# Two cross attentions of a perceiver: the first rebuilt with all heads' queries on partitions, the second reordered around its transposes and maxima

## The reference, cut to what matters

```python
# layer 0: scores = q k / 4 + mask * -1e9, softmax over the 1024 keys, times v, @ Wo.T + bo
qh = split_heads(layernorm(x) @ Wq.T + bq)          # 16 batches, 16 heads, 64 queries, 16 features
kh = split_heads(ctx @ Wk.T + bk)                   # 16 batches, 16 heads, 1024 keys, 16 features
vh = split_heads(ctx @ Wv.T + bv)
attn = softmax(einsum('bhqd,bhkd->bhqk', qh, kh) / sqrt(16) + mask * -1e9)
x = x + merge_heads(einsum('bhqk,bhkd->bhqd', attn, vh)) @ Wo.T + bo
# layer 1: the same without a mask, then causal self attention and an fp4 feed forward
```

## Time and profile before

| | us |
|---|---|
| device time, median of 3 runs | 1369.87 (1366.11 to 1375.72) |
| device time of the profiled execution | 1370.36 |
| its span in the profile | 1368.3 |
| mean granted TensorE clock, as a share of the full one | 0.983 |
| TensorE busy | 1229.0 (90%) |
| VectorE busy | 951.4 (70%) |
| ScalarE busy | 857.8 (63%) |
| POOL busy | 660.1 (48%) |

### The profile page before, as it was taken

The page is one execution under the profiler, slowest core; times in us unless marked ns, Lnnn a source line. Parts: engine busy times, 40 slices in busy tenths (PEclk is TensorE's granted clock), DMA queues, the critical chain, the costliest instruction groups (busy, mean ns, idle before and its releaser), DMA issues. The chain is left out here.

```text
span 1368.3 us, 32530 instructions
## 1 busy us (share of the span) xinstructions
PE 1229.0 (90%) x12656; PEld 887.8 (65%) x12658; DVE 951.4 (70%) x1543; ACT 857.8 (63%) x1373; POOL 660.1 (48%) x897
## 2 busy tenths in 40 slices
PE   6999999999999988897978999998889998988886
PEld 3666767676777765554645667676667676766654
DVE  3787886787777773684676776676756677756674
ACT  3766767667777754543546667676768676767331
POOL 1665555455565642340013446355654657746533
PEclk9999999999999999999999999999999999999998
DMA  4311322111112203001633021002001132000000
GB/s 157 100 55 55 124 61 77 55 56 55 55 56 85 95 2 115 1 1 31 200 115 88 32 63 54 32 33 63 32 33 54 45 81 64 32 2 2 5 9 19
DMA packets 32853, 78.49 MB, mean 57 GB/s; under 512 B 4416, under 2 KB 16448, under 8 KB 28480
## 3 DMA queue, kind: packets, MB, share of 16 engines
q1 hardware_dynamic: 32704, 76.42, 18.2%
HBM read 69.07 MB, written 7.34 MB: 56 GB/s over the span
## 5 line engine op out<-in xcount | busy, mean ns | idle before, releaser
L697 POOL TENSOR_TENSOR ca_fold<-ca_probT 128x512 f32<-128x512 f32 x128 | 164.0, 1281 | 235.9 <-ACT ca_probT L927 235.4
L936 ACT ACTIVATE ca_probT<-bank 128x512 f32<-128x512 f32 x256 | 140.2, 595 | 110.8 <-PE bank L830 109.5
L801 PE MATMUL bank<-ca_kT,ca_q_blk 32*128 32x512 f32 x512 | 146.4, 648 | 9.7 <-DVE ca_probT L1016 7.1
L830 PE MATMUL bank<-ident,ca_prob 128*128 128x128 f32 x1024 | 144.5, 282 | 11.0 <-DVE ca_picked L1028 5.3
L807 PE MATMUL bank<-ca_q_blk,ca_kT 32*128 32x128 f32 x2048 | 150.9, 286 | 0.0
L927 ACT ACTIVATE ca_probT<-ca_probT 128x1024 f32<-128x1024 f32 x128 | 135.5, 1059 | 18.1 <-DVE ca_probT L1016 12.1
L739 PE MATMUL bank<-ca_ctxT,ca_wk 128*128 128x512 f32 x256 | 123.1, 606 | 9.1 <-DMA ca_bk<-in_L_xattn_bk 9.1
L847 PEld LDWEIGHTS bank<-ca_probT,ca_v 128*32 128x32 f32 x4096 | 109.8, 111 | 32.6 <-issue 26.7
L755 PE MATMUL bank<-wv,ctxT 128*128 128x256 f32 x512 | 129.6, 382 | 1.1 <-ACT fw_upT L383 0.6
L830 PEld LDWEIGHTS bank<-ident,ca_prob 128*128 128x128 f32 x1024 | 109.8, 141 | 31.2 <-DVE ca_picked L1028 7.2
L847 PE MATMUL bank<-ca_probT,ca_v 128*32 128x128 f32 x4096 | 126.9, 276 | 3.3 <-issue 1.8
(11 more groups left out here) (324 smaller groups left out, 2606.1 us busy)
## 6 DMA issues: line engine op xcount, KB each, us to landing
ca_ctxT<-in_ctxT SPq DMA_DIRECT2D x16, 1024.0 KB, 5.2
ctxT<-in_ctxT SPq DMA_DIRECT2D x16, 1024.0 KB, 4.7
ca_mask_i<-in_mask SPq DMA_DIRECT2D x32, 256.0 KB, 6.3
ek_ctxT<-in_ctxT SPq DMA_DIRECT2D x12, 512.0 KB, 5.6
early_k<-ek_out SPq DMA_DIRECT2D x48, 128.0 KB, 3.5
ca_kT<-early_k SPq DMA_DIRECT2D x12, 512.0 KB, 5.8
ca_mask_col_i<-in_mask_keys SPq DMA_DIRECT2D x16, 256.0 KB, 6.4
lat<-in_x SPq DMA_DIRECT2D x1, 1024.0 KB, 4.9
```

Of the source, the lines that this page charges most:

```text
L697: pool.tensor_tensor(f[:, :, :], p[:, 0:4, :], p[:, 4:8, :], ALU.add).then_inc(self.fold_step, 1)
L801: mm = pe.matmul(self.core.bank[:, 2 + half, :], self.q_blk[rows, b % 2, u, :, :], self.kT[rows, b % 2, u, :], start=True, stop=True, tile ...
L830: tr = pe.transpose(self.core.bank[:, x, n * P:(n + 1) * P], self.prob[:, s % 2, (4 * h + n) * P:(4 * h + n + 1) * P], self.core.ident[:, :])
L936: self.banks.free(act.activation(self.probT[:, n % 2, 4 * h:4 * h + 4, 2 * (s % 2) + 1, :], self.core.bank[:, x, :].rearrange("p (n q) -> ...
```

## The change

1. The first layer uses a new class `RowAttention`. All four heads go by rows: `scores` is four matmuls of 32 rows and 512 columns on the four row groups of the array, into banks 0 to 3. `maxima` takes two masked maxima on VectorE (the instruction of L988, twice). `exponentials` runs twice on ScalarE. VectorE inverts the row sums (`inverse`), POOL multiplies the exponentials by them (`normalise`, 128x1024, twice per step). Sixteen transposes per step instead of eight, in two portions; the first portion is copied out by VectorE, the second by ScalarE. The column maxima, the two small transposes, the subtraction, the column exponential, the column sums and the sum matmuls are gone, and so are the mask in key order (one 256 KB load and one conversion per batch) and `join_heads`.
2. In the first layer VectorE takes the values and adds their bias; `times_v` comes at even steps from step 4 on, directly behind `scores`, one pair of steps later than before. Banks are handed out in turn over 4, 5, 6, 7.
3. In the second layer `CrossAttention` stays, with three rotating banks. TensorE: the first part of the value projection comes directly behind `scores`, then half of the transposes, `turn_column_max`, the other half, the second part of the values, `spread_top`. The latent transposes of the causal attention come behind `spread_top`.
4. VectorE in the second layer: `tops` comes ahead of `row_maxima`.
5. ScalarE in the second layer: the causal exponential and `take_v` come directly behind `exponentials`, ahead of the other woven work.
6. The fp4 weight preparation in the second layer is spread over other steps (`FW_AT`, `FW_SCALE`, `FW_TRANSPOSE`), and its second and third loads come at batches 6 and 11 instead of 5 and 10.

```diff
@@ class RowAttention (new), the parts that the prediction speaks of
+    def normalise(self, pool, s):
+        for p in range(2):
+            x = 2 * (s % 2) + p
+            pool.wait_ge(self.inv_ready, 2 * s + p + 1)
+            pool.tensor_tensor(self.prob[:, x, :], self.prob[:, x, :], self.inv_sum[:, x:x + 1].broadcast_to([P, CTX]),
+                               ALU.mult).then_inc(self.norm_ready, 1)
...
+        if s >= 1:
+            pe.wait_ge(self.max_ready if self.masked else self.exp_done, 2 * s)
+        for half in range(2):
+            for j in range(2):
+                rows = slice(S * half + 32 * j, S * half + 32 * j + 32)
+                mm = pe.matmul(self.core.bank[:, 2 * j + half, :], self.q_blk[rows, b % 2, u, :, :],
+                               self.kT[rows, b % 2, u, :], start=True, stop=True, tile_position=(S * half + 32 * j, 0))
...
+    def transposes(self, pe, s, p):
+        pe.wait_ge(self.norm_ready, 2 * s + p + 1)
+        for h in range(2):
+            x = self.banks.open(pe, ("t", s, p, h))
...
+    def take_v(self, dve, n):
...
+        self.banks.free(dve.tensor_tensor(self.v[:, b % 2, 2 * i:2 * i + 2, :],
+                                          self.core.bank[:, x, :].rearrange("p (r d) -> p r d", r=2),
+                                          self.bv[:, :].unsqueeze(1).broadcast_to([P, 2, D]), ALU.add), ("v", n))
...
+    def inverse(self, dve, s, p):
+        y = 2 * (s % 2) + p
+        dve.wait_ge(self.exp_done, 2 * s + p + 1)
...
+        dve.reciprocal(self.inv_sum[:, y:y + 1], self.row_sum[:, y:y + 1]).then_inc(self.inv_ready, 1)
@@ first_layer
-        banks = Banks(core, sem)
+        banks = Banks(core, sem, range(4, 8))
-        ca = CrossAttention(core, 0, True, banks, given, sb, sem)
+        ca = RowAttention(core, 0, True, banks, given, sb, sem)
@@ first_layer, vector
             for s in range(STEPS + 3):
...
+                    ca.maxima(dve, s)
+                    ca.inverse(dve, s, 0)
+                if s % 2 == 0 and s >= 4:
+                    ca.take_pv(dve, s // 2 - 2)
+                if s + 2 < STEPS:
+                    ca.take_v(dve, s + 2)
+                if 1 <= s <= STEPS:
+                    ca.take_t_on_vector(dve, s - 1, 0)
                 if s < STEPS:
-                    ca.below_tops(dve, s)
+                    ca.inverse(dve, s, 1)
@@ second_layer, tensor
             for s in range(STEPS):
                 ca.scores(pe, s)
-                if s >= 1:
-                    ca.transposes(pe, s - 1)
-                for t in tile_at(s, 3):
-                    sa.latent_transposes(pe, t, norm1.xn_ready)
                 if s + 2 < STEPS:
                     ca.project_v(pe, s + 2, parts=(0,))
+                if s >= 1:
+                    ca.transposes(pe, s - 1, (0,))
                 ca.turn_column_max(pe, s)
+                if s >= 1:
+                    ca.transposes(pe, s - 1, (1,))
                 if s + 2 < STEPS:
                     ca.project_v(pe, s + 2, parts=(1,))
                 ca.spread_top(pe, s)
+                for t in tile_at(s, 3):
+                    sa.latent_transposes(pe, t, norm1.xn_ready)
@@ second_layer, scalar
                 ca.exponentials(act, s)
+                for t in tile_at(s, 7):
+                    sa.exponentials(act, t)
+                if s + 2 < STEPS:
+                    ca.take_v(act, s + 2)
                 for t in tile_at(s, 3):
                     sa.take_latents(act, t)
-                for t in tile_at(s, 7):
-                    sa.exponentials(act, t)
...
-                if s + 2 < STEPS:
-                    ca.take_v(act, s + 2)
@@ second_layer, vector
                 ca.column_maxima(dve, s)
+                ca.tops(dve, s)
                 ca.row_maxima(dve, s)
-                ca.tops(dve, s)
                 ca.below_tops(dve, s)
```

316 lines of the change are left out of this document (275 added, 41 removed).

## The result

| | us |
|---|---|
| kernel after, median of 4 runs | 1541.57 (1534.46 to 1545.41) |
| kernel before, beside it, median of 4 runs | 1369.56 (1366.11 to 1375.72) |
| ratio, 95% interval | 1.124 (1.118 to 1.131) |
| profiled execution after | 1544.25, span 1542.5 |

The kernel is 12.4% slower: the direction was forecast, the size was not (1441, range 1400 to 1480).

What follows compares the result with a forecast made beforehand. The prediction took TensorE's row of pieces plus its waits to bound the kernel. From the profiled 1370.4 us, -7 for the first layer and +78 for the second layer's bank waits gave 1441 us, range 1400 to 1480.

Steps and rivals of the forecast that it cites:

- First layer: First layer: loop +3 us, start -5, end -5, together -7.
- the mechanism: Second layer, three rotating banks: the keys wait for ScalarE's copy of the values, 1.85 us.
- the plain step: Second layer with keys: odd step 7.9 to 8.05 us (6.24 before), even 10.0 (8.1 before).
- 1.5 x 36 = +54: Second layer, 36 steps with keys: waits for the value copy cost 1.5 us per step, +54 us.
- Mean 0.85: +24: Second layer, 28 steps without keys: even ones 8.25 against 6.7 us, odd ones 0 to 1.6 more; +24 us.
- the centre: Whole kernel: the central forecast, 1441 us, with no cost for a falling clock in it; chance 0.69.
- Rival B: Second layer: the new waits lower TensorE's clock too, 25 to 40 steps paying +32 to +52 us, 1473 to 1493; chance 0.12.
- spares waits at the spread: Second layer, VectorE: earlier `tops` shortens waits at the spread; small, put into the mean costs per step, no own size.
- A (no cost): Second layer, steps with keys: value copy ready when the keys want the bank, kernel not slower, 1353 us; chance 0.05.
- C: First layer slower: scores run in pairs at 1.72 us, +46 us more, 1487; chance 0.03.
- D: Second layer: half the bank's price, copy earlier or steps without keys lose nothing, +35 to +45, 1400 to 1412 us; chance 0.08.

Runs made afterwards that it cites:

- the base: The new first layer (RowAttention) with the second layer wholly as in the kernel before: 1361.32 us, ratio 0.993 (0.991 to 0.995) to the kernel before.

## Why the prediction was wrong, point by point

**First layer: right.** -7 was forecast, step 0 of the second layer starts at 725.2 instead of 732.1. Its parts: loop +2.3 (forecast +3), with 3.05 us of idle TensorE (5 forecast); start -5.2 (-5); end -4.0 (-5). Odd steps 6.46 (6.42), plain pairs 14.80 (14.61), the normalisation 1.90 (1.90), step 4 at 54.8 (55). The scores take 1.07, between my 1.00 and the 1.12 that the Trainium skill's figure for four row tiles (TensorE: Matmul & The Clock Gate, Measured speedup vs the span model) gave; the trace settles it at neither. Alone, against the kernel before, the new first layer measured 1361.3 against 1372.5; the two profiles put 7 of these 11 us there.

**Second layer, the mechanism and the plain step: right.** Keys behind values by three, waiting for L911: forecast 1.85 us, measured 1.90; odd plain steps forecast 7.9 to 8.05, measured 8.17; even ones forecast 10.0, measured 10.27 where the clock stayed full. Value first and keys in bank 4 show it is that wait.

**Second layer, the mean per step: the first error.** The prediction put "1.5 x 36 = +54" and "Mean 0.85: +24" for the 28 steps without keys. The waits grew by 112 us instead of 78: TensorE's idle time, taken step by step from the traces of after and before, grew by 64 us in the steps with keys and by 48, twice the forecast, in those without. For those the sum took 1.55 us in even steps, where `times_v` opens the third bank behind the values, and 0 to 1.6 in odd ones. But pieces of the causal attention open it too, even steps such as step 28 wait 4.1 us, and the places 4, 5 and 7 of each eight make 37 of the 48. The table has the growth of each of the eight positions, from the starts of the steps in the traces of after and of the base, summed over the loop (the slow clock is in it):

```
step mod 8      0     1     2     3     4     5     6     7
us          +21.1 +26.0 +18.3  +9.3 +40.5 +24.9 +16.0 +26.9
```

I carried the plain step over to all steps. In position 4, from step 12 on, ScalarE has two table loads on the way to the value copy, so the wait is 2.2 us longer still: TensorE's idle time grew by 3.2 us a step there, and the step by 2.5 to 6.3 with the slow clock. Before, the longest wait of TensorE for ScalarE in the middle of these steps was 0.6 us. Position 7 has, from step 23 on, the two loads for the feed forward's norm (waits of 2.8 us). In position 1, from step 17 on, the causal exponential stands between the row exponential and the value copy (waits of 2.8 to 3.2 us), as in step 25 of the kernel after:

```profile
993.36 1.04 ACT L2373 ACTIVATE ek_out<-ek_out 128x1024 f32<-128x1024 f32 x1
```

The step that failed was to price the heavy steps, and those without keys, by the plain one, without reading ScalarE's row in each kind of step up to the value copy; the rows for it were in the trace of before, as in its step 20, whose scores start at 882.23:

```profile
884.89 1.28 ACT L1854 ACT_TABLE_LOAD   x1
...
887.52 1.28 ACT L919 ACT_TABLE_LOAD   x1
```

**Second layer, the clock: the second error, and twice as large.** The prediction said of the clock "I keep the centre without it" and gave Rival B 0.12 with +32 to +52. It measured +71 as the growth of busy time, more than the rival's highest price, and about 52 of them came back when the idle time was filled. I had read a fall of the clock behind 1.85 us of idling and worked out waits of 1.85 for most steps; then the fall belonged in the centre. Nearly the same wait in steps 7 and 8 of the kernel after (the granted clock is the third number from the end):

```profile
783.64:789.85 6.21, 4.35 (x41) 3.47 (x38) 5.19 (x8) 3.44 (x6) 3.27 (x6) 1.00 0.00 0
789.89:791.80 1.91, 1.91 (x4) 0.67 (x4) 0.00 (x0) 0.00 (x0) 0.00 (x0) 1.00 0.05 9
791.80:798.15 6.35, 4.36 (x40) 3.51 (x39) 4.49 (x6) 5.31 (x8) 2.69 (x4) 1.00 0.00 0
798.15:801.73 3.58, 3.58 (x5) 1.09 (x5) 1.33 (x1) 0.00 (x0) 0.00 (x0) 0.52 0.00 0
801.73:803.83 2.10, 2.10 (x78) 2.01 (x77) 0.00 (x0) 1.88 (x3) 0.00 (x0) 1.00 0.00 0
```

After 1.90 us of idling in step 7 the keys run 1.91 us at 1.00, TensorE's upper level; after 1.99 us in step 8 they take 3.58 us at 0.52, the lower one. Waits of 1.90 to 1.99 went either way in other steps too, so the length of the last wait alone doesn't decide.

**`tops` early: the lateness right, its price too low.** I counted half a microsecond of lateness in the wait, and taking it back shortens the plain wait from 1.90 to 1.29 us. But this brings 34 us of clock beside 27 of idle time (56 us of the kernel, the fp4 places included), and alone in the old order it costs 29 us. That it "spares waits at the spread" is nothing that a run shows as a gain.

**The sum.** 1370.4 - 7 + 112 + 71 = 1546, against 1544.25 of the profiled execution. So of the 103 us between the forecast and the profiled execution 34 are waits (112 for 78) and 71 the clock (71 for 0), within 2 us.

**The rivals.** A (no cost) is out. B was right in kind and too low: the clock fell as well, and cost 71 us, not 32 to 52. C is out (scores 1.07, not 1.72). D is out: steps without keys lost more than counted, not less.

**What stays open.** The parts don't add: TensorE's old order with everything else new measured 1390, the same as `tops` early alone; 29 and 6 should have given 1397. Of the 41 us by which the new order with the value copy first stays behind the base, the waits named above are seen, but no run takes them away. Why 1.99 us of idling drops the clock in one step and not in another isn't settled.

## What to carry to other kernels

When banks are handed out in turn, moving one piece changes who waits for whom three openings on: list for each opening the reader it waits for and that reader's place on its own engine, in every kind of step, the heavy ones first, and not only in the plain one. Repeated waits of about 2 us on TensorE cost here two thirds as much again in clock (112 and 71 us), so that cost belongs in the centre; moving the reader (here one copy past one exponential) is worth more than moving the matmuls. And judge such a reordering step by step, not by its sum: the value copy first lost 8 us over all steps and gained 9 in the quarter of them where it belongs.

## What the runs showed of the hardware

- Useless matmuls in idle time made the kernel 40 us faster: 57 us of extra work on TensorE, mean granted clock of the loop from 0.89 to 0.97. Of such idling the Trainium skill says that cycling through PSUM banks can leave TensorE idle between groups often enough for its clock gate to oscillate (TensorE: Matmul & The Clock Gate, A second HAM failure mode: psum-queue depth-cycling); this case agrees, with 0.52 behind one wait and 1.00 behind the next.
- A stay at the lower level was short: 0.52 over 3.58 us, and 1.00 again for the 2.10 us of `times_v` behind it. The cost in this step was 3.58 - 1.91 = 1.67 us, near the wait itself.
- Four fp32 matmuls of 32 rows and 512 columns, one on each row group, took 1.07 us. One matmul of 512 columns on all 128 rows takes 0.86 (half of the keys' 1.72 in the earlier trace rows); if one of 32 rows took as long by itself, which no run shows, the four would be 4 x 0.86 / 1.07 = 3.2 times as fast as one after the other.
